# Wavelet filter over 256 images on one Trainium2 core: two rows of either half per partition, and the row transform in 64x32 tiles for two images at a time

## The reference

```python
yl, yh = _dwt2(x, 4)                                    # 42x42 at the coarsest level
yl_out = jnp.einsum('bixy,ioxy->boxy', yl, w_yl)
yh_out = yh[:-1] + [jnp.einsum('bicxy,iocxy->bocxy', yh[-1], w_yh)]
return _idwt2(yl_out, yh_out)                           # 8 x 32 x 512 x 512
```

## Time and profile before

| what | value |
|---|---|
| profiled execution | 2077.18 us |
| its span, first to last instruction | 2075.2 us |
| median of the three timed runs | 2116.64 us |
| mean granted TensorE clock | 0.986 |
| PE, DVE, ACT busy | 91%, 40%, 22% of the span |
| moved by DMA | 827.16 MB, mean 399 GB/s |

### The profile page before, as it was taken

How to read it: one execution, slowest core, us unless ns; L and a number is a source line. 1 busy time by engine, 2 the same in 40 slices (tenths; PEclk the granted TensorE clock), 3 DMA queues, 4 the chain that set the end, 5 groups by cost and what they waited for, 6 DMA issues and landing times.

```text
span 2075.2 us, 44244 instructions
## 1 busy us (share of the span) xinstructions
PE 1880.7 (91%) x17580; PEld 940.4 (45%) x17580; DVE 828.0 (40%) x947; ACT 460.2 (22%) x1043; POOL 3.6 (0%) x7
## 2 busy tenths in 40 slices
PE   6999999999999779999999999888998888999996
PEld 4656666666666444444333343333343333334332
DVE  1222222222223455555444444444444344444443
ACT  1223222222222452121121121121121111112110
POOL 0000000000000000000000000000000000000000
PEclk9999999999999899999999999999999999999998
DMA  8999999999998877999999999999999999999998
GB/s 351 404 385 417 421 421 422 422 421 422 421 422 360 308 279 304 377 426 427 427 427 427 427 427 427 379 383 394 422 423 392 361 370 373 421 422 420 421 422 367
DMA packets 114794, 827.16 MB, mean 399 GB/s; under 512 B 12752, under 2 KB 13520, under 8 KB 17488
## 3 DMA queue, kind: packets, MB, share of 16 engines
q1 hardware_dynamic: 114768, 826.78, 97.9%
HBM read 558.29 MB, written 268.44 MB: 398 GB/s over the span
## 4 chain that ended last, share of the span: by engine, by line
DMA 54%; PE 9%; SPq 2%; issue 1%; DVE 0%; ACT 0%; DVEq 0%
DMA out<-x_sb 51%; PE ps L472 5%; DMA both<-w_full 2%; SPq L282 1%; DMA x_sb<-x 1%; PE ps L462 1%; PE ps L428 1%; PE ps L423 1%; DMA both<-w_rest 0%; PE ps L452 0%; SPq L277 0%; DVE x_sb L706 0%; SPq L276 0%; DVEq L133 0%; ACT both L596 0%
## 5 line engine op out<-in xcount | busy, mean ns | idle before, releaser
L472 PE MATMUL ps<-spread,const 128*128 128x512 f32 x2048 | 943.6, 604 | 108.9 <-DVE x_sb L706 108.8
L706 DVE TENSOR_TENSOR x_sb<-ps,x_sb 128x1024 f32<-128x1024 f32 x500 | 593.3, 1221 | 666.5 <-DMA x_sb<-x 579.3
L472 PEld LDWEIGHTS ps<-spread,const 128*128 128x128 f32 x2048 | 374.6, 190 | 676.3 <-issue 409.7
L610 ACT COPY spread<-ps 84x512 f32<-84x512 f32 x256 | 148.8, 581 | 967.2 <-PE ps L462 966.8
L336 PE MATMUL ps<-x_sb,const 32*32 32x512 f32 x8192 | 292.4, 606 | 38.0 <-DMA x_sb<-x 32.4
L349 PEld LDWEIGHTS ps<-const,work 128*128 128x128 f32 x2048 | 248.4, 194 | 55.6 <-ACT work L510 41.5
L462 PE MATMUL ps<-const,pick 128*84 128x512 f32 x512 | 261.3, 592 | 0.7 <-issue 0.7
L349 PE MATMUL ps<-const,work 128*128 128x84 f32 x2048 | 257.4, 279 | 3.1 <-ACT work L510 3.1
L510 ACT COPY work<-ps 128x512 f32<-128x512 f32 x256 | 131.4, 600 | 418.4 <-PE ps L336 418.4
L336 PEld LDWEIGHTS ps<-x_sb,const 32*32 32x32 f32 x8192 | 139.5, 103 | 141.0 <-issue 101.5
L655 DVE COPY work<-ps 128x336 f32<-128x336 f32 x256 | 130.0, 508 | 177.1 <-PE ps L349 177.1
(11 more groups left out here) (22 smaller groups left out, 220.8 us busy)
## 6 DMA issues: line engine op xcount, KB each, us to landing
x_sb<-x SPq DMA_DIRECT2D x498, 1024.0 KB, 12.2
out<-x_sb SPq DMA_DIRECT2D x250, 1024.0 KB, 14.2
both<-w_full SPq DMA_DIRECT2D x30, 896.0 KB, 6.5
work<-x SPq DMA_DIRECT2D x6, 1024.0 KB, 9.1
out<-work SPq DMA_DIRECT2D x6, 1024.0 KB, 9.4
both<-w_rest SPq DMA_DIRECT2D x6, 224.0 KB, 3.2
const<-consts SPq DMA_DIRECT2D x1, 888.0 KB, 4.6
```

What stands on the lines that cost most here:

```text
L472: last = nc.tensor.matmul(ps[:, 2 + k], const[:, SH + P * k:SH + P * k + P], spread[:, p], start=True, stop=True)
L610: nc.scalar.copy(spread[0:ROWS, p], ps[0:ROWS, p]).then_inc(s_copied[p], 1)
L706: nc.vector.tensor_tensor(part, ps[:, 2 + 2 * half:4 + 2 * half], part, ALU.add).then_inc(added[half], 1)
```

## The change

An image now lies in its slot with rows 2p and 2p+1 of its upper half (rows 0 to 255) and rows 2p and 2p+1 of its lower half at partition p. Each partition's 8 KiB are in two pieces of 4 KiB in `x` and `out`, for loads and stores alike; the number of DMAs and their bytes are unchanged, and so is their issue order. A segment of 128 rows lies on 64 partitions with 2 rows each, so the row transform is 32 matmuls per group in place of 64, each with 64 contraction rows. `h_stage` is called twice in a group, for images 0 and 1 and for images 2 and 3, with `turn_stage` of images 0 and 1 between the calls; it waits for two loads, and a semaphore for each pair (`h_done`, four in place of two) releases the loads and the copies of two images. ScalarE's copies are split in the same way. The synthesis only has its constants in another order.

```diff
+DUO = 2
...
-        for r in range(ROW_RUN):
-            at = A3H + TILE * r
-            c[part, at:at + NEAR] = a[near, P * g + r:P * g + P:ROW_RUN].T
+        upper = slice(P // 2 * (g % 2), P // 2 * (g % 2 + 1))
+        for r in range(2):
+            at = A3H + TILE * (2 * (g // 2) + r)
+            c[upper, at:at + NEAR] = a[near, P * g + r:P * g + P:2].T
...
-    x_rows = x.rearrange("b i (p r) w -> (b i) p r w", r=ROW_RUN)
-    out_rows = out.rearrange("b i (p r) w -> (b i) p r w", r=ROW_RUN)
+    x_rows = x.rearrange("b i (j p r) w -> (b i) p j (r w)", p=P, r=2)
+    out_rows = out.rearrange("b i (j p r) w -> (b i) p j (r w)", p=P, r=2)
+
+    def paired(image):
+        return image.rearrange("p (j r) w -> p j (r w)", r=2)
...
-        h_done = sems("h_done", HALVES)
+        h_done = sems("h_done", SLOTS // DUO)
...
                 for c in range(SLOTS):
-                    if c % GROUP == 0:
-                        sp.wait_ge(h_done[c // GROUP], t)
-                    sp.dma_start(x_sb[:, c], x_rows[SLOTS * t + c]).then_inc(x_loaded[c], 16)
+                    if c % DUO == 0:
+                        sp.wait_ge(h_done[c // DUO], t)
+                    sp.dma_start(paired(x_sb[:, c]), x_rows[SLOTS * t + c]).then_inc(x_loaded[c], 16)
...
-                sp.dma_start(out_rows[first + c], x_sb[:, c]).then_inc(x_stored[c], 16)
+                sp.dma_start(out_rows[first + c], paired(x_sb[:, c])).then_inc(x_stored[c], 16)
...
-            def h_stage(a, t):
+            def h_stage(a, t, first, duo):
 
                 n = HALVES * t + a
-                for m in range(GROUP):
+                images = (DUO * duo, DUO * duo + 1)
+                for m in images:
                     pe.wait_ge(x_loaded[GROUP * a + m], 16 * (t + 1))
-                pe.wait_ge(h_copied, GROUP * n)
+                if not first or a > 0:
+                    pe.wait_ge(h_copied, GROUP * n + DUO * (duo - 1))
                 pe.sem_inc(h_begun, 1)
-                for r in range(ROW_RUN):
+                for r in range(2):
                     for g in range(SEGS):
-                        part = slice(TILE * g, TILE * g + TILE)
-                        for m in range(GROUP):
+                        part = slice(P // 2 * (g % 2), P // 2 * (g % 2 + 1))
+                        at = A3H + TILE * (2 * (g // 2) + r)
+                        for m in images:
                             to = TILE * ((g + m) % SEGS)
-                            last = nc.tensor.matmul(ps[to:to + TILE, m], const[part, A3H + TILE * r:A3H + TILE * r + TILE],
-                                                    x_sb[part, GROUP * a + m, r], start=r == 0, stop=r == ROW_RUN - 1)
-                last.then_inc(h_done[a], 1)
+                            last = nc.tensor.matmul(ps[to:to + TILE, m], const[part, at:at + TILE],
+                                                    x_sb[part, GROUP * a + m, 2 * (g // 2) + r], start=r == 0, stop=r == 1)
+                last.then_inc(h_done[GROUP // DUO * a + duo], 1)
...
                 for a in range(HALVES):
                     n = HALVES * t + a
-                    h_stage(a, t)
                     before = not first or a > 0
+                    h_stage(a, t, first, 0)
                     if before:
                         w_stage(n - 1, after=batch if a else None)
                     turn_stage(a, t, 0)
                     if before:
                         last_stage(n - 1)
-                    for m in range(1, GROUP):
+                    turn_stage(a, t, 1)
+                    if batch is not None and a == 0:
+                        channels_stage(0, batch)
+                        channels_stage(1, batch)
+                    h_stage(a, t, first, 1)
+                    for m in (2, 3):
                         turn_stage(a, t, m)
```

More of the change, by code:

```diff
@@ L117, in constants @@
     c[:ROWS, SW:SW + SIZE] = back.T
-    for r in range(ROW_RUN):
-        c[:ROWS, SH + P * r:SH + P * r + P] = back[r::ROW_RUN].T
+    for k in range(ROW_RUN):
+        c[:ROWS, SH + P * k:SH + P * k + P] = back[SIZE // 2 * (k // 2):SIZE // 2 * (k // 2 + 1)][k % 2::2].T
     c[:, EYE:EYE + P] = np.eye(P)
@@ L228, in _ @@
             for c in range(SLOTS):
-                sp.dma_start(x_sb[:, c], x_rows[c]).then_inc(x_loaded[c], 16)
+                sp.dma_start(paired(x_sb[:, c]), x_rows[c]).then_inc(x_loaded[c], 16)
             with sp.Fori(1, TURNS) as t:
                 for c in range(SLOTS):
-                    if c % GROUP == 0:
-                        sp.wait_ge(h_done[c // GROUP], t)
-                    sp.dma_start(x_sb[:, c], x_rows[SLOTS * t + c]).then_inc(x_loaded[c], 16)
+                    if c % DUO == 0:
+                        sp.wait_ge(h_done[c // DUO], t)
+                    sp.dma_start(paired(x_sb[:, c]), x_rows[SLOTS * t + c]).then_inc(x_loaded[c], 16)
             def load_w(c, v, weights):
@@ L245, in load_early @@
             def load_early(e):
-                sp.dma_start(early[e], x_rows[IMAGES - 2 * SLOTS + e]).then_inc(early_loaded[e], 16)
+                sp.dma_start(paired(early[e]), x_rows[IMAGES - 2 * SLOTS + e]).then_inc(early_loaded[e], 16)
             for c in range(WBUFS):
@@ L276, in store @@
                 sp.wait_ge(added[1], SLOTS * t + c + 2)
-                sp.dma_start(out_rows[first + c], x_sb[:, c]).then_inc(x_stored[c], 16)
+                sp.dma_start(out_rows[first + c], paired(x_sb[:, c])).then_inc(x_stored[c], 16)
             def refill(c, t, first):
                 sp.wait_ge(x_stored[c], 16 * (t - (c < EARLY)))
-                sp.dma_start(x_sb[:, c], x_rows[first + c]).then_inc(x_loaded[c], 16)
+                sp.dma_start(paired(x_sb[:, c]), x_rows[first + c]).then_inc(x_loaded[c], 16)
             for c in range(SLOTS):
@@ L292, in _ @@
                     sp.wait_ge(added[1], SLOTS + c + 2)
-                    sp.dma_start(out_rows[IMAGES - 2 * SLOTS + c], early[c]).then_inc(early_stored, 16)
+                    sp.dma_start(out_rows[IMAGES - 2 * SLOTS + c], paired(early[c])).then_inc(early_stored, 16)
                 else:
@@ L507, in copy_h @@
             def copy_h(a, t, m):
-                act.wait_ge(h_done[a], t + 1)
+                act.wait_ge(h_done[GROUP // DUO * a + m // DUO], t + 1)
                 nc.scalar.copy(along_h[:, m], ps[:, m]).then_inc(h_copied, 1)
@@ L528, in turn1 @@
                 for a in range(HALVES):
-                    for m in range(GROUP):
-                        copy_h(a, t, m)
+                    copy_h(a, t, 0)
+                    copy_h(a, t, 1)
                     if not first or a > 0:
@@ L533, in turn1 @@
                     if batch is not None and a == 0:
-                        for v in range(STEPS):
+                        copy_m(0, batch)
+                        copy_m(1, batch)
+                    copy_h(a, t, 2)
+                    copy_h(a, t, 3)
+                    if batch is not None and a == 0:
+                        for v in range(2, STEPS):
                             copy_m(v, batch)
```

## The result

The changed kernel is slower by 1.7%: 20 runs beside 20 of the kernel before give a ratio of 1.0166, with an interval of 1.0122 to 1.0211. The medians of all 20 runs are 2127.72 us against 2113.16 us. That is only 15 us more, because the ratio and its interval go by the fast runs alone, those within 1.5% of the fastest run of the same kernel. On the median of before the ratio is +35 us. The profiled execution of the change took 2120.45 us, with a span of 2118.6 us against 2075.2 us, +43 us; but the profiled execution of before (2077.18 us) was one of its quickest, near the lowest of its runs (2075.70 us). So the size of the loss depends on the yardstick: +15, +35 or +43 us.

What follows compares the result with a forecast made beforehand. The prediction took full DMA engines as the bound, in stage 1 with 0.54 us per group to spare. It summed 2077 + 55 - 3 - 5 = 2124 us profiled, +47 us, carried to the median as 2164 us (+2.2%), range 2127 to 2194.

Steps and rivals of the forecast that it cites:

- The packets: Loads and stores, stages 1 and 3: 6080 more packets per engine at 9 ns each, +55 us (ends 0 and +170).
- The issue: SP's issue of loads: as many DMAs in the same order, each with twice the runs, costed at nothing.
- The row transform: TensorE, stage 1: one call for two images takes 2.0 us, between 1.9 and 2.67 us.
- The third turn: TensorE, stage 1: nothing hides ScalarE's first copy behind the second call, 0.7 us of new idle per group.
- TensorE's period: Stage 1, per group: 9.7 us on TensorE (9.5 to 11.1), below the DMAs' 10.2 us.
- Parts 3 and 4: Row transform time and third-turn idle on TensorE, stage 1: cost nothing while TensorE stays below the DMAs; cover 0.5 us per group.
- Release and tail: Stage 1: earlier slot release closes the hole near the start, -3 us; shorter work after the last load, -5 us.
- a packet without a price: Loads and stores: packets cost nothing beside their bytes, only release and tail act, 2109 us; chance 0.21.
- TensorE as the bound of stage 1: Each row transform call keeps its 0.95 us, period 11.1 us against 10.2: +57 us on top, 2221 us; chance 0.10.
- The price of the weight packets: Loads and stores: each added packet costs 28 ns, +170 - 8 us, 2279 us; chance 0.06.
- The fourth rival: Stage 3: slow stretches go away with addresses 4 KiB apart per partition and packets free, 41 us gained, 2068 us; chance 0.13.

Runs made afterwards that it cites:

- Compute alone: The changed kernel with the access patterns of x and out put back, every load and store in one 8 KiB run per partition: 0.9866 of before, some -28 us.

## Why the prediction was right, point by point

The forecast, slower by some 2% through the price of packets, came true: +1.7% against +2.2%. In microseconds it was 2164 us against 2127.72 us, at the very edge of its own range (2127 to 2194 us). Of these 36 us some 3 come from the median of before, which over more runs is 2113 us and not 2117; 12 are the distance from +47 to +35 us, and the other 20 the distance between the ratio and the medians.

1. **The packets.** In stage 1 the price taken was 9 ns and the measured one is 9.1 ns: 256 x 73 ns = +19 us. That it fits so well is partly luck, since 9 ns was a choice between 0 and 28 ns. In stage 3 it was mis-sized: 4.4 ns, so 250 x 70 ns = +18 us where 36 were in the sum, and 421 GB/s where "some 415" was the sign. The +55 us are +36 us. The upper bound of 28 ns from the weight packets was not met anywhere; that it was a thin queue's, as argued, no run tested. The figure that the prediction gave beside the sum, 408.7 GB/s by the Trainium skill ("DMA: Bandwidth & Descriptors", "iDMA fabric"), was good: this trace has 410 GB/s in stage 1.
2. **The issue** of the loads cost nothing, as costed.
3. **The row transform** takes 1.88 us per call; 2.0 was taken. The pace of issue would explain it, but no run varied that pace alone.
4. **The third turn** waits 0.75 us; 0.7 was taken.
5. **TensorE's period** is 9.81 us, predicted 9.7, below the DMAs' 10.24, predicted 10.2. Parts 3 and 4 are hidden.
6. **Release and tail.** The tail gave the 5 us. The holes gave more than the 3 us taken: the first 150 us run at 379 GB/s before, of 422, and at 402 after, of 410; that is 15 us lost against 3, so -12 us. One hole of 2 us had been read; there were several between 36 and 150 us, and the prediction did not see that TensorE's granted clock stood at 0.50 just ahead of the first. How much of the 12 us is the clock's and how much that of the earlier release, no run separates. Compute alone, at -28 us, agrees with the sum of both terms, -17 us, within its interval (-46 to -10 us).

The terms that the traces bear out thus add up to 36 - 12 - 5 = +19 us. The sum of +47 us stood 28 us above them: 19 us too much for the packets, nearly all in stage 3, and 9 us too little gained at the start. That it came within 12 us of the measured +35 us is luck: some 16 us are in that figure which no term of the prediction has and no run explains. Beside the 15 us between the medians the terms alone are enough, and the sum is 32 us too high.

The rivals: a packet without a price is refuted (389, 410 and 422 GB/s at 2, 4 and 8 KiB). TensorE as the bound of stage 1 did not come, with 0.4 us per group to spare. The price of the weight packets did not come. The fourth rival, that the new addresses make the slower slices go away, did not come: the changed kernel's trace has them too, 67 us of them. Loads in two DMAs at the old addresses lost as much as 4 KiB loads at the new ones, which speaks for the cutting of one side and against the addresses.

## What to carry to other kernels

Where the DMA engines are full, count packets as well as bytes: an arrangement that halves the contiguous run must gain more than 7 to 9 ns per added packet and engine in pure loading (4 to 5 ns, at most 6, with loads and stores mixed) before it pays. A faster TensorE stage buys nothing behind full DMA engines; here it only filled the holes of the start and shortened the tail. Where loads and stores share a queue, try the size of the stores' DMAs by itself: it gained 2.0% on the kernel before and nothing on the changed one. And where one profiled execution stands beside another, look first where each lies among the runs of its kernel.

## What the runs showed of the hardware that was not expected

- At a full share, loads and stores mixed drop for hundreds of microseconds from 427 GB/s (before) or 421 (changed) to some 340 to 394. In these two traces loads alone did not, after the start (422 or 410 in every slice).
- Cutting only the loads in two (1.0250) or only the stores (0.9795) moves the time by 4.5% between them, at nearly the same full rate (423 and 422 GB/s from 1000 to 1250 us). The Trainium skill ("DMA: Bandwidth & Descriptors", "Rules for kernel authors") advises against splitting a transfer into partition halves, since both run on the same engines. For these stores the measurement decides otherwise: 0.9795, interval 0.9747 to 0.9843.
- An added packet costs about half as much when loads and stores are mixed (4.4 and 4.8 ns at the same addresses) as with loads alone (7 and 9 ns).
